# Two units of probability-times-value matmuls back to back, in a two-layer attention kernel

## The reference

```
x = x + L0(gn(x))      # L0: softmax(q k / 4 + rel_h + rel_w) v over all 1024 positions
x = x + L1(gn(x))      # L1: softmax(q k / 4, 7x7 neighbourhood mask, 16 register keys) v
```

## Time and profile before

| | |
|---|---|
| median of 3 runs | 4923.62 us (4919.65 to 4926.85) |
| the profiled execution | 4917.51 us, its span 4915.8 us |
| PE busy | 4495.7 us (91%) |
| DVE busy | 3081.0 us (63%) |
| ACT busy | 2606.4 us (53%) |
| POOL busy | 892.4 us (18%) |
| granted TensorE clock | 0.952 of full speed on average |

### The profile page before, as it was taken

The page is one execution under the profiler, slowest core; times in us unless marked ns, Lnnn a source line. Parts: engine busy times, 40 slices in busy tenths (PEclk is TensorE's granted clock), DMA queues, the critical chain, the costliest instruction groups (busy, mean ns, idle before and its releaser), DMA issues.

```text
span 4915.8 us, 97560 instructions
## 1 busy us (share of the span) xinstructions
PE 4495.7 (91%) x32598; PEld 2289.2 (47%) x32598; DVE 3081.0 (63%) x5558; ACT 2606.4 (53%) x3955; POOL 892.4 (18%) x1899
## 2 busy tenths in 40 slices
PE   3979999999999999999999999999999999999998
PEld 2334453544535455454544535445453544535444
DVE  2736657566675656657566675656657566675644
ACT  1443646555564555646555564555646555565564
POOL 3122021122102212021122102212021121102111
PEclk7887999999999999999999999999999999999998
DMA  6333253432424433244432424434144432424401
GB/s 122 85 68 75 47 109 76 99 79 59 95 56 99 94 71 85 44 106 80 99 79 55 93 62 99 94 69 88 44 108 79 99 79 52 96 62 99 87 14 39
DMA packets 235881, 386.25 MB, mean 79 GB/s; under 512 B 58396, under 2 KB 133728, under 8 KB 235360
## 3 DMA queue, kind: packets, MB, share of 16 engines
q1 hardware_dynamic: 189280, 266.13, 23.7%
q10 hardware_dynamic: 21504, 75.51, 7.7%
q0 software_dynamic: 24576, 37.80, 4.8%
HBM read 227.79 MB, written 88.08 MB: 64 GB/s over the span
## 4 chain that ended last, share of the span: by engine, by line
PE 74%; DVE 10%; issue 5%; DMA 4%; SPq 4%; ACT 2%; DVEq 0%; POOL 0%; ACTq 0%
PE P L1123 14%; PE P L1141 14%; PE P L1085 13%; PE P L948 7%; PE P L949 6%; DVE mx L891 6%; PE P L1061 5%; PE P L1173 4%; PE P L1194 4%; PE P L1093 3%; DMA QA<-queries 2%; DVE mxc L897 1%; PE P L1166 1%; DMA biases<-xn 1%; PE P L1211 1%
## 5 line engine op out<-in xcount | busy, mean ns | idle before, releaser
L891 DVE TENSOR_REDUCE mx<-P 128x1 f32<-128x512 f32 x3072 | 1924.0, 683 | 436.3 <-PE P L1085 432.9
L761 ACT ACTIVATE probs<-P 128x1024 f32<-128x1024 f32 x1536 | 1507.0, 1022 | 781.3 <-PE P L1141 780.8
L1085 PE MATMUL P<-K,AR 96*128 96x256 f16 x6144 | 1100.0, 283 | 15.4 <-DVE mx L891 6.2
L1141 PE MATMUL P<-AR,K 113*128 113x512 f16 x3072 | 921.8, 382 | 4.1 <-DMA AR<-mrow 2.9
L897 DVE TENSOR_REDUCE mxc<-P 128x1 f32<-128x336 f32 (+1 forms) x1536 | 649.4, 475 | 307.9 <-PE P L1094 304.4
L777 ACT ACTIVATE probs<-P 128x320 f32<-128x320 f32 (+3 forms) x1632 | 617.2, 436 | 411.3 <-PE P L1194 334.5
L1123 PE MATMUL P<-probs,V 128*17 128x512 f32 x6144 | 811.8, 600 | 9.9 <-ACT probs L761 9.9
L1085 PEld LDWEIGHTS P<-K,AR 96*128 96x128 f16 x6144 | 540.4, 99 | 546.7 <-DVE mx L891 209.5
L1141 PEld LDWEIGHTS P<-AR,K 113*128 113x128 f16 x3072 | 216.1, 98 | 662.8 <-ACT probs L761 520.4
L1194 PE MATMUL P<-A,K 113*128 113x320 f16 (+2 forms) x1536 | 444.5, 305 | 13.6 <-ACT probs L777 12.8
L1093 PE MATMUL P<-K,A 112*128 112x320 f16 (+1 forms) x1536 | 403.4, 298 | 53.8 <-DVE mx L891 36.4
(11 more groups left out here) (120 smaller groups left out, 3704.2 us busy)
## 6 DMA issues: line engine op xcount, KB each, us to landing
AR<-biases SPq DMA_DIRECT2D x384, 256.0 KB, 7.8
AR<-queries ACTq DMA_DIRECT2D x96, 512.0 KB, 5.8
biases<-xn SPq DMA_DIRECT2D x192, 256.0 KB, 3.0
AR<-queries ACTq DMA_DIRECT2D x96, 256.0 KB, 8.5
K<-oraw POOLq DMA_DIRECT2D x384, 64.0 KB, 4.8
xin<-in_x_dram SPq DMA_DIRECT2D x16, 768.0 KB, 10.5
queries<-oraw SPq DMA_DIRECT2D x384, 32.0 KB, 4.8
QA<-queries SPq DMA_DIRECT2D x192, 64.0 KB, 5.2
```

The source lines that it names most:

```text
L761: nc.scalar.activation(probs[:, u % RING, j:j + 2, :], P[:, b:b + 2, :], ACT.Exp).then_inc(p_done[0], 1)
L891: V_.reduce_max(mx[:, n // 2, n % 2:n % 2 + 1], bank, AX.X).then_inc(used, 1)
L1085: last = mm(bank[:, QD * (v % 2):QD * (v % 2) + QD], AR[0:ROWS_MAX[0], part % SLOTS, v, c, j, 128 * q:128 * q + 128], K0[0:ROWS_MAX[0], h, ...
L1141: last = mm(P[:, j, :], K0[0:ROWS, h, 128 * kt:128 * kt + 128], AR[0:ROWS, p % SLOTS, kt // 2, :, j, :], start=True, stop=True)
```

## The change

Three things. First, the values of units u - 1 and u are issued together after the scores of unit u, for odd u in layer 0, and for even u from 2 in layer 1 (unit 0 by itself after unit 1). Second, the one-hot rows are split: the 4 DMAs into `K0` (`static_keys`) are issued between the queries of group 0 and those of groups 1 and 2, and the other 28 behind the fill of phase 1. The first maxima wait only for the four. The first 20 maxima of phase 0 go ahead of the `rel` jobs of group 1 in both `first_phases`. Third, image 0's 33 jobs of phase 1 move from the stage ahead of its main into the main, and the 25 jobs of group 1 of the last layer-1 stage move into its main as well.

```diff
 def plan_l0(image, i1, n0):
-    placed = evenly(max_jobs(0, image, 2)[EARLY:], 0, 20)
+    if is_image(image, 0):
+        placed = evenly(max_jobs(0, image, 1), 0, 13) + evenly(max_jobs(0, image, 2), 13, 28)
+    else:
+        placed = evenly(max_jobs(0, image, 2), 0, 20)
@@ plan_l1
-        return plan(STEPS[1], evenly(max_jobs(1, image, 2), 5, 60) + last)
+        placed = evenly(max_jobs(1, image, 2), 34 if i0 is None else 5, 62)
+        return plan(STEPS[1], placed + last + (evenly(max_jobs(1, image, 1), 0, 28) if i0 is None else []))
@@ first_phases
-                   *rel_jobs(image, 1), fill(image, 2), *early_maxes(image), *more)
+                   *first[:20], *rel_jobs(image, 1), fill(image, 2), *first[20:], *more)
@@ block_stages
-        yield "jobs", 1, i1, in_turn(*max_jobs(1, i1, 0), *max_jobs(1, i1, 1))
+        yield "jobs", 1, i1, in_turn(*max_jobs(1, i1, 0))
@@ moves
+                    if part == 1 and is_image(image, 0):
+                        static_rows()
@@ run_job
-                        pe.wait_ge(rows_in, ROWS_IN)
-                        pe.wait_ge(out_in, 16)
+                        pe.wait_ge(keys_in, KEYS_IN)
@@ attend_global
-                    if u:
+                    if u % 2:
                         use(u - 1)
-                use(UNITS[0] - 1)
+                        use(u)
@@ attend_local
-                    if full:
+                    if u == 1:
                         use(full - 1)
-                use(UNITS[1] - 1)
+                    elif u and u % 2 == 0:
+                        use(full - 1)
+                        use(full)
```

More of the change, by code:

```diff
@@ L165, in plan_l1 @@
     placed += [(28, ask(n0, 2)), (28, fill(n0, 2))]
-    placed += evenly(early_maxes(n0), 25, STEPS[1] - TAIL)
+    placed += evenly(max_jobs(0, n0, 0) + max_jobs(0, n0, 1), 25, STEPS[1] - TAIL)
     return plan(STEPS[1], placed + last)
-def early_maxes(image):
-    return max_jobs(0, image, 0) + max_jobs(0, image, 1) + max_jobs(0, image, 2)[:EARLY]
 def first_phases(image, *more):
+    first = max_jobs(0, image, 0)
     return in_turn(*[ask(image, p) for p in range(SLOTS)], *rel_jobs(image, 0), fill(image, 0), fill(image, 1),
-                   *rel_jobs(image, 1), fill(image, 2), *early_maxes(image), *more)
+                   *first[:20], *rel_jobs(image, 1), fill(image, 2), *first[20:], *more)
 def block_stages(i0, i1, n0):
@@ L199, in block_stages @@
     else:
-        yield "jobs", 0, n0, first_phases(n0, *stat_jobs(1, i0))
+        yield "jobs", 0, n0, first_phases(n0, *max_jobs(0, n0, 1), *stat_jobs(1, i0))
 def before_loop():
@@ L339, in attention_kernel @@
         SUM_STEPS, POOL_STEPS = 3 * TT - 2, 3 * TT - 2 + 5
-        ROWS_IN = (8 + NH - 1 + 12) * 16
+        ROWS_IN, KEYS_IN = (4 + NH - 1 + 12) * 16, 4 * 16
         w_in = sems("w_in")
@@ L346, in attention_kernel @@
         rows_done = sem("rows_done")
-        rows_in = sem("rows_in")
+        rows_in, keys_in = sem("rows_in"), sem("keys_in")
+        onehot_done = sem("onehot_done")
         tr_done = sem("tr_done")
@@ L442, in _, with static_keys @@
                         sp.dma_start(rnat[32 * j:32 * j + REG, :], regs).then_inc(tab_in, 16)
+            def static_keys():
+                sp.wait_ge(onehot_done, 1)
+                for r, n in ((0, 0), (1, 0), (32, 1), (33, 1)):
+                    sp.dma_start(K0[r:r + 2 * D - 1:2, :, :],
+                                 oneh[0:D, n:n + 1, :].broadcast_to((D, NH, S))).then_inc(keys_in, 16)
             def static_rows():
                 sp.wait_ge(rows_done, 1)
-                for r, n in ((0, 0), (1, 0), (32, 1), (33, 1)):
-                    sp.dma_start(K0[r:r + 2 * D - 1:2, :, :],
-                                 oneh[0:D, n:n + 1, :].broadcast_to((D, NH, S))).then_inc(rows_in, 16)
                 for r, n in ((48, 0), (80, 1)):
@@ L497, in operands_out @@
                         query_blocks(im, 0)
+                    if g == 1 and is_image(im, 0):
+                        static_keys()
                     for s, (t, ready) in enumerate(((HI, hi_done), (LO, lo_done))):
@@ L533, in stage @@
                         rows_to_operands(sp, L, im, 0, ((A1, 0, HI), (A1, 16, HI), (A1, 32, LO)), q_in)
-                    if L == 0 and is_image(im, 0):
-                        static_rows()
                 if kind == "main" and L == 0 and not is_image(im, B - 1):
@@ L614, in static_rows @@
                                                         pattern=pat, channel_multiplier=1))
+                    if n == 1:
+                        chained(nc.gpsimd.memset(scratch[:, 4:5], 0.0))
+                        nc.gpsimd.memset(scratch[:, 4:5], 0.0).then_inc(onehot_done, 1)
+                        pool.wait_ge(onehot_done, 1)
                 R = WIN // 2
@@ L1112, in attend_global @@
                 y_read()
+                if is_image(im, 0):
+                    pe.wait_ge(rows_in, ROWS_IN)
+                    pe.wait_ge(out_in, 16)
                 def use(u):
```

1 line of the change is left out of this document (removed).

## The result

| | before | after |
|---|---|---|
| median of 4 runs each | 4924.74 us (4919.65 to 4926.85) | 5056.91 us (5055.36 to 5064.60) |
| ratio, 95% interval | | 1.0271 [1.0255, 1.0286] |
| span of the profiled execution | 4915.8 us | 5056.3 us |
| granted clock | 0.952 | 0.949 |

The kernel is 2.7% slower. The page of the changed kernel: work and shares of the chain that ended last, then the maxima and the exponentials of layer 0 with DVE's and ACT's idle time ahead of them.

A forecast was written before the change was run, and what follows sets the result against it. PE carries most of the chain, but pairing makes it wait for DVE's three-bank stock of maxima or ACT's exponentials. 134 + 45 + 7 - 26 + 20 - 9 = +171 on 4917.5 gives 5088, rounded to 5090 us; range 4990 to 5145.

The forecast's parts named there:

- The sum, +171: Whole kernel: all terms together add 171 us to the profiled execution's 4917.5, giving 5088, rounded to 5090 us.
- What bounds a pair: Main stages: DVE's stock of three maxima binds dense pairs (6.29 us); ACT's chain of four exponentials binds others (5.63).
- Dense pair, +0.45: Layer-0 main, two units with eight maxima: 6.29 us for 5.84, with one DVE pause of 1.3 for two of 0.43.
- Pairs on ACT's chain, 5.63: Layer-0 pairs that DVE does not bind take 5.63 us: seven maxima +0.10, layer-1 jobs +0.45, no jobs +1.41.
- The mixed pairs, 1.0 together: Six layer-0 pairs (`rel` jobs, both kinds of maxima, last pair): each 0 to 0.45 us, taken as 1.0 per main stage.
- The third rival: PE stands idle in pairs without jobs, the granted clock falls to 1.2 GHz; sum passes 5150 us; clock or worse 0.08.
- Layer-0 mains, +134: Layer-0 main stages of images 1 to 15: 8.9 us more each over 24 pairs, +134 us together.
- Layer 1, +45: Layer-1 mains of images 0 to 13: a DVE pause of 0.45 in about eight pairs, 3.2 us each, +45 together.
- the +7: Layer-1 mains of images 14 and 15, where ACT leads: a pair takes 4.0 us for 3.72, +7 together.
- Image 0's start, -26: First image, split one-hot writes and moved maxima: layer-0 main starts at about 138 and not 164.07, -26 us.
- Image 0's main, +20: Image 0's layer-0 main takes up the moved maxima: first 28 steps 52.7 us against 44.5 (+8), with the rest +20.
- The last image, -9: Last image: the second run of maxima leaves the chain, its row costs +2, PE's jobs beside ACT 0 to 4: -9.

The follow-up runs named there:

- the short maxima: Kernel before with layer-0 maxima over 128 of 512 columns and exponential arguments scaled by 0.1: 4721.54 us in the old order, 4757.78 us with layer-0 values in pairs.
- the split: Kernel before with layer-0 values in pairs, except units 2 and 3, whose values are issued one by one: 5027.08 us, ratio 1.0221.

## Why the prediction was right, and where its sizes were off

- **The sum, +171: +132 by the medians.** The direction and the mechanisms are right, and most terms are too large.
- **What bounds a pair: right, both mechanisms.** Dense pairs lose on DVE's pause (the short maxima turn -0.33 into a gain of 0.21), pairs without maxima on ACT's chain (shortening both turns the pairing of layer 0 into a gain of 45 us).
- **Dense pair, +0.45: measured +0.33.** The time to the next score step was 1.84 behind the first value and not 1.88, and the eight maxima took 4.87 and not 4.99: only the first of a run takes 0.67, the others 0.60. The layout had 0.65 for the first and 0.62 for each other.
- **Pairs on ACT's chain, 5.63: measured 5.51 and 5.45.** Four exponentials in a row took 3.77, not 3.89. With layer-1 jobs that is +0.27 for the +0.45 predicted, in five pairs. A copy after a phase adds 0.5 there (5.95 against 5.46), as forecast (0.6).
- **The mixed pairs, 1.0 together: the step that failed.** "Each costs between 0 and 0.45" was bounded by the wrong rows, since four `rel` jobs in one pair form a chain that neither price describes. That one pair cost +1.9 in the mean, 29 us over images 1 to 15, most of it by the lower clock (0.74 to 0.88). The third rival (the clock falls as well) was placed in pairs without jobs; it came true here. The reason given against it, a clock of 1.00 in main stages, doesn't hold everywhere: before, this very pair stands at 0.91 to 0.92 in 4 of the 15 images, and steps 22 to 29 of the layer-1 mains at 0.60 to 0.86 in all 14.
- **Layer-0 mains, +134: +104.5.** The too high prices above and the missed 1.9 partly cancel: 7.0 a main for 8.9. That part of the hit is luck.
- **Layer 1, +45: +37.5, for the reason given.** That is 2.7 an image and not 3.2, and all of it lies in the stretch with a maximum per step: steps 30 to 35 went from 4.05 to 4.95, steps 36 to the end from 41.31 to 43.11. In the latter DVE stands idle for 8.0 us and not 6.6. The steps with `rel` jobs (22 to 29) went from 16.26 to 16.06. (Both orders have issued the same values at these borders.) Image 14's +4.2 and the paired part of image 15 (9.7 less the 4.8 that the jobs cost there) make 9.1 for the +7.
- **Image 0's start, -26: -27.2, by luck.** The biases left at 87.6 and not 77, the fill came 4.9 behind them and not 8.0, and the first maxima's matmuls began at 99.75 and not 93. None of this set the start of the main: the maxima were done at 125.4, and SP came to their row at 131.57, behind its other work. That work, as the prediction said, is the 28 writes, but they began at 98.3 and not 90, and took 23.9 and not 33: two errors that cancel.
- **Image 0's main, +20: +25.2.** Its first 28 steps took 61.9 and not 52.7 (44.5 before), and the rest 7.8 more for the 12 predicted. Without pairs the first 28 steps already take 14.6 more, where the term had 8 with them.
- **The last image, -9:** -11.4 in the jobs stage, but the moved jobs cost 4.8 in the main and not 0 to 4: -6.6.

## What to carry to other kernels

When a change batches one kind of work to save switches, count what the other engines hold in stock (banks, buffers) over the doubled block; here three banks last one block of values and not two, and 0.22 saved met 0.55 of new waiting (the 0.33 lost and the 0.22). Price the odd places of a loop one by one, above all where small dependent jobs stand in a row: one pair of 24 held 29 of the 104.5 us that layer 0's mains lost, and most of that was the clock. To tell the clock from the order, compare images of one kernel, in which the order is fixed. And when a kernel misses by a fixed amount in each turn of a hardware loop, look at the first instructions behind the jump before looking at the edit.

## What the runs showed of the hardware that was not expected

- One instruction less on PE ahead of a hardware loop came with 3.8 to 4.0 us more for each turn (49.4 and 52.5 over 13), in two kernels of fourteen; the cause is argued and not shown. The transposes at the lower clock are 1.2 to 1.7 of it.
- TensorE's clock fell to 1.2 GHz inside a stretch where PE counts as 90% busy (11.77 of 13.01), after pauses of 0.77 and 0.47 among jobs of 64 columns. With the same order of work it fell in 7 of 15 images and stayed in 8 (the split), which made 1.6 us of difference.
- Sixteen small DMAs issued right behind four long writes took 22.2 us to issue, ahead of them 10.4. From the issue of the biases to that of their fill it took 14.5 right behind the writes, and 4.9 and 8.0 in the changed kernel and before.
